# Eight resident Toeplitz tiles in a decoder layer's state-space mixer, with the selects, the row stores and the entry loads re-ordered

## The chip, the cores and the metric

One core of one Trainium2 chip runs the whole layer in one launch. The metric is device time in microseconds, from the run's own clock; lower is better. The engines are called as in the profile: PE (TensorE matmul), DVE (VectorE), ACT (ScalarE), POOL (GpSimd) and SP (SyncE, which only issues transfers here). All arithmetic is fp32 or fp32r.

## What is computed

The input x is 4 sequences of 1024 tokens by 256 channels. The layer has three blocks, each with a layer norm ahead and a residual behind it: a diagonal state-space mixer, cross attention to 64 context rows per sequence, and a feed-forward part (256 to 1024, two 1024 by 1024 layers, back to 256).

```python
def mixer(x):                                  # residual + (scan output) @ W_out.T + b_out
    xn = (x - mean) / sqrt(var + 1e-5) * ln_gamma + ln_beta
    dA = exp(-exp(log_A) * dt[:, None]); dB = B_param * dt[:, None]     # (256, 64)
    def step(h, u):
        h = dA * h + dB * u[..., None]
        return h, einsum('dn,bdn->bd', C_param, h) + D_param * u
    ys = scan(step, 0, xn)
    return x + einsum('btd,ed->bte', ys, W_out) + b_out
x = x + mixer(layernorm(x))
x = x + attention(ctx, ctx, layernorm(x))
x = x + ffn(layernorm(x))
```

## The kernel before

The scan is done in chunks of 64 steps (L = 64, 16 chunks a sequence, 64 columns in all). For each of the 256 channels (128 on the upper and 128 on the lower half of the partitions) there are three small products: `state` multiplies the tokens of a chunk by the channel's entries EE (64 x 64 powers of the decay) and gives what the chunk adds to the state; `within` multiplies the tokens by a 64 x 64 lower Toeplitz tile TT of the channel's convolution kernel; `carried` multiplies the scanned states by GG and adds them to the same output. Sixteen channels of each half are a group (GRP = 16, NGRP = 8), eight are a round (`OCT` = 8, 16 rounds); DVE runs the scan over the chunks of a round (L431).

**Preparation (0 to about 51 us).** DVE builds the powers GG by six doublings (L337), PE sums each column of GG over the 64 states with a row of ones (L461, four rounds v into four banks, each emptied by ACT, L277), and the sums, the convolution kernel, go to DRAM (`kernel_rows`, L175, eight stores of SP). From there SP loads the Toeplitz tiles: one transfer per half and group, 64 partitions that each read 4 KB one element further on (L141, `tt_load`). The entries come in the same way from `alpha_rows` (L146, `entries_load`) and ACT makes exponentials of them (L289). POOL clears what is above the diagonal of a Toeplitz tile with two selects a group (L211, `mask`). The tokens are normed twice over: DVE takes the statistics (L343, L346), POOL the power -0.5 (L240, L244), ACT and DVE scale and shift 20 and 12 columns of each half of the tokens (L284, L370), and DVE multiplies by gamma and adds beta in eight parts (L379, L384; `PARTS`), three of them ahead of the first product, the rest between the scans.

**Core (about 53 to 102 us).** PE goes through rounds o = 0 to 16. In a round it does state(o+1), within(o) and carried(o-1), 48 matmuls (96 records in the trace). Before round o it waits for: the selects of the group (`t_mask`), the exponentials (`e_rdy`), three, four, six and eight parts of the tokens (`z_b`), the scan of the round before (`h_scan`) and free output banks (`y_out`). Between the scans DVE does one gamma or beta pass a round up to o = 8. ACT empties the outputs (L304) and makes the residual bases (L292), to which POOL adds the bias `bo` (L216, needs `wo_in`, the landing of `bo` and `woT`).

**Order of the transfers.** One queue, SP's, issues nearly all: x, the two alpha stores, the tokens, gamma and beta, EE of groups 0 and 1, `bo`, `woT`, the row stores (each waits for ACT's copy), three small weights, then, once all rows are in DRAM (`kr_st`), TT of groups 0 to 3, EE of groups 2 to 7, the context rows. TT of groups 4 to 7 go into the same four buffers of `ring` and are each issued when PE has finished with the group four before (`w_ps`). POOL's queue runs: pow, pow, selects of group 0, pow, selects of groups 1 to 3, small masks, clearing of the value rows (L867), then `gpsimd_core` with selects 4 to 7 and the biases.

**Rest.** After the core PE turns and projects the outputs, takes part in the first attention block and runs the feed-forward loop (159 to 932 us); the weights are loaded in the shadow of this once the last state product is done (`h_ps`, L191 to L200). The change does not touch it.

Of the kernel before, what the change touches and what calls it, by code (L numbers as in the profile page):

```python
# [32 lines left out]
P = 128  # L33
BATCH, T, DM = 4, 1024, 256
N = 64
# [19 lines left out]
ACT_SHARE = 20  # L55
# [3 lines left out]
def mixer_parts(nc, ctx, a, t):  # L59
# [7 lines left out]
    def sem(name):  # L67
# [12 lines left out]
    ones = sb("ones", [P, 32], "c")  # L80
# [22 lines left out]
    dtc = sb("dtc", [P, 4], "d")  # L103

    TT = [ring[:, 1024 * k:1024 * (k + 1)] for k in range(4)]
    ksb = ring[:, :].rearrange("p (a m) -> p a m", a=8)
# [7 lines left out]
    kps = [[pair[k][:, 512 * h:512 * (h + 1)] for h in range(2)] for k in (2, 0)]  # L114
# [4 lines left out]
    x_in, E_in, xr_in = ([sem(f"m_{n}{g}") for g in range(8)] for n in ("x_in", "E_in", "xr_in"))  # L119
    const, exps, coef, al_st, coef_t, pk_done, g_row, d_add = (  # L120
        sem("m_" + n) for n in ("const", "exps", "coef", "al_st", "coef_t", "pk_done", "g_row", "d_add"))
    k_ps, k_ev, kr_pad, e_rdy, t_mask = (sem("m_" + n) for n in ("k_ps", "k_ev", "kr_pad", "e_rdy", "t_mask"))
    kr_st = sem("m_kr_st")
    T_in = [sem(f"m_T_in{k}") for k in range(4)]
# [24 lines left out]
    def sync_mixer(e):  # L149
# [20 lines left out]
        for v in range(4):  # L170
            for h in range(2):
                u = 2 * v + h
                e.wait_ge(k_ev, u + 1)
                c = (1 - h) * (P * L) + v * 2048
                e.dma_start(kr[0, c:c + 2048].rearrange("(q m) -> q m", q=4), ksb[0:P:32, u, :]).then_inc(kr_st, 16)  # L175
        for n in ("xW", "keys", "scl"):
            e.dma_start(t[n], a[n]).then_inc(k_in, 16)
        e.wait_ge(kr_st, 128)
        e.wait_ge(kr_pad, 16)
        for g in range(4):  # L180
            tt_load(e, g)
        for g in range(2, NGRP):
            entries_load(e, g)

    def sync_core(e):
        for g in range(4, NGRP):
            e.wait_ge(w_ps, 2 * (g - 4) + 2)
            tt_load(e, g)
# [4 lines left out]
        e.wait_ge(w_d, 48)  # L193
        for n in ("w1", "w2", "w3"):
            e.dma_start(t[n].bitcast(F32), t["d" + n]).then_inc(w_in, 16)
# [22 lines left out]
    def gpsimd_prep(e):  # L218
        e.memset(ident[:, :], 0.0).then_inc(const, 1)
        e.memset(rev[:, :], 0.0).then_inc(const, 1)  # L220
        e.memset(ones[:, :], 1.0).then_inc(const, 1)
# [4 lines left out]
        e.wait_ge(const, 6)  # L226
        e.affine_select(out=ident[:, :], in_=ident[:, :], compare_op=ALU.not_equal, fill=1.0, base=0,
                        pattern=[[-1, P]], channel_multiplier=1).then_inc(const, 1)
        for h in range(2):
            blk = rev[64 * h:64 * h + 64, 64 * h:64 * h + 64]  # L230
            e.wait_ge(const, 7 + h)
            e.affine_select(out=blk, in_=blk, compare_op=ALU.not_equal, fill=1.0, base=-63,
                            pattern=[[1, 64]], channel_multiplier=1).then_inc(const, 1)
        e.wait_ge(const, 9)
        e.dma_start(kr[:, DM * L:DM * L + L], rev[0:1, L:2 * L]).then_inc(kr_pad, 16)

        for b in range(2):
# [3 lines left out]
        mask(e, 0)  # L241
        e.wait_ge(t_mask, 2)
        e.wait_ge(nat_v, 1)
        e.tensor_tensor(rsm[:, :], svn[:, :], mhalf[:, :], ALU.pow).then_inc(natural, 1)  # L244
        e.wait_ge(natural, 1)
        for g in range(1, 4):
            mask(e, g)
        e.wait_ge(t_mask, 8)

    def gpsimd_core(e):  # L250
        e.wait_ge(wo_in, 32)
        done = 0
        for g, until in ((4, 0), (5, 0), (6, 0), (7, 4), (None, TILES)):
            for tile in range(done, until):
                bias(e, tile)
            done = until
            if g is not None:
                e.wait_ge(base_b, done)
                mask(e, g)
                e.wait_ge(t_mask, 2 * g + 2)  # L260

    def scalar(e):
# [11 lines left out]
        def row_evac(v):  # L274
            e.wait_ge(k_ps, v + 1)
# [17 lines left out]
        for v in range(4):  # L293
            row_evac(v)
        e.wait_ge(const, 9)
        norm_apply(0)
        entry_exp(0)
        norm_apply(1)
        for g in range(1, 3):
# [21 lines left out]
    def vector(e):  # L321
        e.wait_ge(exps, 2)
# [8 lines left out]
        for row in (0, N):  # L331
            e.tensor_copy(edit[row:row + 1, 1, :], wT[row:row + 1, :]).then_inc(d_add, 1)
# [6 lines left out]
        def stats(first, until):  # L339
            for j in range(first, until):  # L340
                if j % 4 == 0:
                    e.wait_ge(xr_in[j // 4], 16)
                e.bn_stats(stn[:, j, :], xres[:, j, :]).then_inc(stat, 1)  # L343
                if j % SB >= 2:
                    e.wait_ge(stat, j - 1)
                    e.bn_aggr(mvn[:, j - 2, :], stn[:, j - 2, :]).then_inc(aggr, 1)  # L346

        def variances(b):
            for j in (SB * b + SB - 2, SB * b + SB - 1):
                e.wait_ge(stat, j + 1)  # L350
                e.bn_aggr(mvn[:, j, :], stn[:, j, :]).then_inc(aggr, 1)
            e.wait_ge(aggr, SB * b + SB)
# [37 lines left out]
        stats(4, 8)  # L390
        double(5)
        e.wait_ge(d_in, 32)
# [1134 lines left out]
```

## Time and profile before

| | us |
|---|---|
| median of 3 runs | 935.07 (934.67 to 935.14) |
| the profiled execution | 934.08 |
| its span, first to last instruction | 932.3 |
| preparation, to the first `within` product | 53.0 |
| core, 53.0 to 102.4 | 49.4 |
| turn, project, first attention block, to 158.9 | 56.5 |
| feed-forward loop, to 932.3 | 773.4 |

The page has the busy share of each engine in 40 slices of 23.3 us: PE is at 99% from the sixth slice on, and below it in the first three, which hold the preparation and the core. The time line gives instructions in order of time with the idle time before them in square brackets; the chain of waits follows the end of the program back to what released each step, and "issue" in it is time for which the profile shows no cause. The windows give busy time, granted clock of TensorE, share of the 16 DMA engines and GB/s for a stretch.

### The profile page before, as it was taken

How to read it: one execution, taken by the hardware profiler on the slowest of the kernel's cores; microseconds unless marked ns; L12 is line 12 of the kernel's file. 1: busy time of each engine (PE TensorE's matmuls, PEld its weight loads, DVE VectorE, ACT ScalarE, POOL GpSimd, SP SyncE). 2: the span in 40 equal slices, each digit the busy share in tenths (PEclk: the TensorE clock that was granted, in tenths of full speed). 3: DMA queues.
4: the chain of work that ended last, by engine and by line, in shares of the span. 5: the costliest groups of instructions: out<-in, count | busy, mean ns of one | idle time of the engine just before them, and what ended most of it. 6: DMA issues, size and time to landing. Idle time of an engine off the chain costs nothing.

```text
span 932.3 us, 15096 instructions
## 1 busy us (share of the span) xinstructions
PE 869.6 (93%) x5570; PEld 697.0 (75%) x5570; DVE 514.6 (55%) x927; ACT 493.6 (53%) x761; POOL 183.2 (20%) x201
## 2 busy tenths in 40 slices
PE   1168999899999999999999999999999999999997
PEld 0068867677777778777877887778778777777886
DVE  7987485465446464555555555554555456553411
ACT  2927533476356735764475536653575366635432
POOL 1567800500041002200230014000500050003000
PEclk9679999999999999999999999999999999999999
DMA  9961797500110002000200010001100110001000
GB/s 340 243 162 55 261 387 306 226 1 1 52 45 0 0 22 73 0 0 15 81 0 0 0 73 22 0 0 51 45 0 0 51 45 0 0 23 45 1 1 25
DMA packets 15497, 61.79 MB, mean 66 GB/s; under 512 B 2835, under 2 KB 4502, under 8 KB 14646
## 3 DMA queue, kind: packets, MB, share of 16 engines
q1 hardware_dynamic: 15430, 61.31, 19.0%
q8 instruction: 24, 0.39, 0.2%
q14 instruction: 11, 0.09, 0.0%
q0 software_dynamic: 32, 0.00, 0.0%
HBM read 49.63 MB, written 23.20 MB: 78 GB/s over the span
## 4 chain that ended last, share of the span: by engine, by line
PE 89%; DVE 5%; issue 4%; ACT 1%; POOL 0%; DMA 0%; SPq 0%; DVEq 0%; POOLq 0%
PE pair L1342 51%; PE pair L1329 11%; PE pair L1354 6%; PE pair L1269 4%; PE pair L1280 3%; PE pair L1296 3%; PE pair L470 2%; PE pair L477 2%; PE pair L1289 1%; PE pair L1319 1%; PE pair L1236 1%; PE pair L484 1%; PE pair L539 1%; DVE GG L337 1%; DVE stn L343 1%
## 5 line engine op out<-in xcount | busy, mean ns | idle before, releaser
L950 ACT ACTIVATE vbuf<-pair,scl 128x512 f32<-128x512 f32 x128 | 87.8, 686 | 231.0 <-PE pair L1342 222.1
L1342 PE MATMUL pair<-h2hi,h_turned 128*128 128x512 f32 x512 | 202.6, 396 | 0.0
L1342 PE MATMUL pair<-h2lo,h_turned 128*128 128x512 f32 x512 | 199.6, 390 | 0.0
L1342 PE MATMUL pair<-h1hi,h_turned 128*128 128x512 f32 x384 | 153.1, 399 | 0.0
L1342 PE MATMUL pair<-h1lo,h_turned 128*128 128x512 f32 x384 | 150.0, 391 | 0.0
L1118 DVE TENSOR_TENSOR h1lo<-vbuf,h1hi 128x512 fp32r<-128x512 f32 x80 | 57.7, 722 | 120.1 <-ACT h1hi L951 119.3
L1342 PEld LDWEIGHTS pair<-h2hi,h_turned 128*128 128x128 f32 x512 | 96.2, 188 | 25.2 <-issue 5.9
L1342 PEld LDWEIGHTS pair<-h2lo,h_turned 128*128 128x128 f32 x512 | 96.2, 188 | 19.3
L1118 DVE TENSOR_TENSOR h2lo<-vbuf,h2hi 128x512 fp32r<-128x512 f32 x64 | 44.2, 691 | 107.2 <-ACT h2hi L951 107.1
L1329 PE MATMUL pair<-zThi,w_turned 128*128 128x512 f32 x224 | 92.0, 411 | 2.9 <-DVE vbuf L1142 2.9
L1142 DVE SCALAR_TENSOR_TENSOR vbuf<-pair,scl,sg 128x512 f32<-128x512 f32 x64 | 47.9, 750 | 80.5 <-ACT sg L939 60.8
L1342 PEld LDWEIGHTS pair<-h1hi,h_turned 128*128 128x128 f32 x384 | 72.1, 188 | 24.5 <-issue 10.5
L1329 PE MATMUL pair<-zTlo,w_turned 128*128 128x512 f32 x224 | 88.6, 396 | 0.0
L903 ACT ACT_TABLE_LOAD x65 | 83.4, 1283 | 1.1
L843 POOL TENSOR_TENSOR lnv<-lnv 128x4 f32<-128x4 f32 x16 | 16.3, 1017 | 342.8 <-DVE lnv L1023 320.4
L1342 PEld LDWEIGHTS pair<-h1lo,h_turned 128*128 128x128 f32 x384 | 72.2, 188 | 14.1
L875 POOL TENSOR_TENSOR h1lo<-vbuf,h1hi 128x512 fp32r<-128x512 f32 x48 | 61.9, 1290 | 79.6 <-ACT h1hi L942 79.6
L939 ACT ACTIVATE sg<-pair,scl 128x512 f32<-128x512 f32 x64 | 44.0, 687 | 58.9 <-PE pair L1329 57.7
L470 PE MATMUL pair<-tok,EE 64*64 64x60 f32 x512 | 38.7, 278 | 25.9 <-DVE tok L384 24.4
L1329 PEld LDWEIGHTS pair<-zThi,w_turned 128*128 128x128 f32 x224 | 42.6, 190 | 17.7 <-DVE vbuf L1142 7.4
L857 POOL TENSOR_TENSOR kblk<-keys,hmask 128x256 f32<-128x256 f32 x18 | 10.7, 616 | 207.6 <-PE pair L1269 207.6
L1342 PE MATMUL pair<-h1hi,w_turned 128*128 128x512 f32 x128 | 50.4, 394 | 0.0
(145 smaller groups left out, 1593.3 us busy)
## 6 DMA issues: line engine op xcount, KB each, us to landing
h_turned<-d_h SPq DMA_DIRECT2D x2, 4096.0 KB, 15.1
xres<-in_x SPq DMA_DIRECT2D x8, 512.0 KB, 7.5
tok<-in_xs SPq DMA_DIRECT2D x8, 512.0 KB, 12.2
EE<-alpha_rows SPq DMA_DIRECT2D x16, 256.0 KB, 10.7
ring<-kernel_rows SPq DMA_DIRECT2D x16, 256.0 KB, 4.3
xr<-x_rows SPq DMA_DIRECT2D x8, 512.0 KB, 3.5
out<-xr SPq DMA_DIRECT2D x16, 256.0 KB, 2.1
x_rows<-xres SPq DMA_DIRECT2D x7, 512.0 KB, 12.4
```

The costliest lines, as they stand in the source:

```text
L470: ins = e.matmul(out, EE[L * h:L * h + L, i, :], rhs, start=True, stop=True)
L875: e.tensor_tensor(h1[1][:, m, :], vb[:, m % 2, :], h1[0][:, m, :], ALU.subtract).then_inc(S["lo"], 1)
L903: e.activation(warm[:, 1:2], warm[:, 0:1], function).then_inc(S["warm"], 1)
L939: e.activation(sg[:, m % 2, :], pair[m % 2][:, 0:512], ACT.Silu, scale=sc1[:, m:m + 1]).then_inc(S["sg_rdy"], 1)
L950: e.activation(vb[:, s % 2, :], h_ps[s % 4], ACT.Gelu, scale=sc)
L1118: e.tensor_tensor(dst[1][:, n % HC, :], vb[:, n % 2, :], dst[0][:, n % HC, :], ALU.subtract).then_inc(S["lo"], 1)
L1142: e.scalar_tensor_tensor(vb[:, m % 2, :], pair[m % 2][:, 512:1024], sc2[:, m:m + 1], sg[:, m % 2, :], ALU.mult, ALU.mult).then_inc(S["v_rd ...
L1269: ins = e.matmul(pair[2][:, g * BLK + b * 256:g * BLK + (b + 1) * 256], qa[64 * g:64 * g + 64, h, tile * P:(tile + 1) * P], kblk[64 * g:64 ...
L1280: ins = e.transpose(pair[3][:, b * BLK + r * P:b * BLK + (r + 1) * P], unit(j, u)[:, r // 2, c:c + P], ident[:, :])
L1329: ins = e.matmul(pair[m % 2][:, 512 * g:512 * g + 512], w[:, k, m * P:(m + 1) * P], zT[part][:, k * BLK:(k + 1) * BLK], start=(k == 0 and ...
L1342: ins = e.matmul(bank, w[:, k, m * P:(m + 1) * P], src[part][:, k, :], start=(k == 0 and part == 0), stop=(k == HC - 1 and part == 1))
L1354: ins = e.matmul(h_ps[m], h1T[:, k, m * P:(m + 1) * P], h1[part][:, k, :], start=(k == 0 and part == 0), stop=(k == HC - 1 and part == 1))
```

## The change

- **Eight resident tiles.** TT of groups 4 to 7 get buffers of their own in the space of the weights w1 and w2, so no TT load waits for PE. All eight groups are loaded before the core. The loads of w1 to w3 into SBUF wait for the last `within` product.
- **SP's order.** EE of groups 0 to 3 are loaded ahead of the row stores; then TT 0, 1, 2, EE 4, TT 3, EE 5, TT 4, EE 6, TT 5, EE 7, TT 6, TT 7; `bo`, `woT` and the three small weights stand behind all of them.
- **POOL's order.** All selects move into `gpsimd_core`, behind its wait for `wo_in` and a new one for the third gamma pass (`z_h`), ahead of all biases and of the value rows' clearing. POOL also takes over the two one-row additions of D to GG and the two one-row copies back from DVE.
- **Kernel rows.** A weight `pick` with one column of ones places the four rounds in four rows of the same two banks, so PE does its 32 matmuls without a wait, ACT copies two tiles in place of eight, and stores eight times from its own queue, in the middle of its first norm pass (`ROWS_AT` = 3).
- **Work shared otherwise.** ACT takes the statistics of tiles 8 to 15 (two passes with an accumulated output, L295 and L301 of the changed kernel) and 18 in place of 20 columns of a norm pass, DVE 14 in place of 12. DVE clears the state banks at the start and does norms(1) after two whole parts of the tokens. All three first exponentials come after both norm passes. PE does five 128 x 512 matmuls (L497 of the changed kernel) after the second beta pass, ahead of the first state product, whose result is not used.

POOL's queue from the second pow to the value rows, before (`ring` holds TT, `rsm` and `rn` are the powers, the names in brackets the semaphores waited for):

```order
L240 TENSOR_TENSOR rn<-sv,mhalf 128x16 [waits m_sv_rdy] x2
L211 AFFINE_SELECT ring<-ring 64x1024 [waits m_t_mask,m_T_in0]
L211 AFFINE_SELECT ring<-ring 64x1024 [waits m_t_mask]
L244 TENSOR_TENSOR rsm<-svn,mhalf 128x32 [waits m_nat_v,m_t_mask]
L211 AFFINE_SELECT ring<-ring 64x1024 [waits m_t_mask,m_T_in1,m_natural]
```

and now:

```order
L250 TENSOR_TENSOR GG<-GG,edit 1x128 [waits m_g_row,m_w_row,m_d_in]
L250 TENSOR_TENSOR GG<-GG,edit 1x128
L244 TENSOR_TENSOR rn<-sv,mhalf 128x16 [waits m_sv_rdy,m_d_add]
L256 COPY GG<-edit 1x128 [waits m_powd,m_k_ps]
L256 COPY GG<-edit 1x128
L244 TENSOR_TENSOR rn<-sv,mhalf 128x16 [waits m_sv_rdy,m_g_back]
L261 TENSOR_TENSOR rsm<-svn,mhalf 128x32 [waits m_powd,m_nat_v]
```

```order
L213 AFFINE_SELECT ring<-ring 64x1024 [waits m_xr_T_in0,m_z_h,m_t_mask,m_wo_in,f_mk]
L213 AFFINE_SELECT ring<-ring 64x1024 [waits m_t_mask]
L213 AFFINE_SELECT ring<-ring 64x1024 [waits m_t_mask,m_xr_T_in1]
```

The first select has moved behind all three powers and waits for `m_wo_in` too, which it did not before.

SP's queue from the entries to the context rows, before:

```order
L146 DMA EE<-alpha_rows 64x1024 [waits m_al_st]
L146 DMA EE<-alpha_rows 64x1024 x3
L168 DMA bo<-in_ab 128x256
L169 DMA woT<-in_aW 128x512
L175 DMA kernel_rows<-ring 4x512 [waits m_k_ev] x8
L177 DMA xW<-in_xW 128x512
L177 DMA keys<-in_keys 128x512
L177 DMA scl<-in_scl 128x34
L141 DMA ring<-kernel_rows 64x1024 [waits m_kr_pad,m_kr_st]
L141 DMA ring<-kernel_rows 64x1024 x7
L146 DMA EE<-alpha_rows 64x1024 x12
```

and now (`tt_82` and `tt_83` are the buffers of groups 4 to 7):

```order
L154 DMA EE<-alpha_rows 64x1024 x7
L149 DMA ring<-kernel_rows 64x1024 [waits m_kr_pad,m_kr_st]
L149 DMA ring<-kernel_rows 64x1024 x5
L154 DMA EE<-alpha_rows 64x1024 x2
L149 DMA ring<-kernel_rows 64x1024 x2
L154 DMA EE<-alpha_rows 64x1024 x2
L149 DMA tt_82<-kernel_rows 64x1024 x2
L154 DMA EE<-alpha_rows 64x1024 x2
L149 DMA tt_82<-kernel_rows 64x1024 x2
L154 DMA EE<-alpha_rows 64x1024 x2
L149 DMA tt_83<-kernel_rows 64x1024 [waits m_nat_v]
L149 DMA tt_83<-kernel_rows 64x1024 x3
L184 DMA bo<-in_ab 128x256
L185 DMA woT<-in_aW 128x512
```

`bo` and `woT` have gone from ahead of the row stores to behind 24 transfers of 256 KB that wait for the rows.

The diff, cut to what the text speaks of:

```diff
-ACT_SHARE = 20
+ACT_SHARE = 18
+ACT_STATS = (8, 16)
+ROWS_AT = 3
+PAD = L
...
-    kps = [[pair[k][:, 512 * h:512 * (h + 1)] for h in range(2)] for k in (2, 0)]
+    kps = [pair[2][:, 512 * h:512 * (h + 1)] for h in range(2)]
...
-        for g in range(2):
+        for g in (0, 1, 2, 3):
             entries_load(e, g)
+        e.wait_ge(kr_st, 128)
+        e.wait_ge(kr_pad, 16)
+        for g in range(NGRP):
+            if g == 6:
+                e.wait_ge(nat_v, 1)
+            tt_load(e, g)
+            if g in (2, 3, 4, 5):
+                entries_load(e, g + 2)
         e.dma_start(bo[:, :], a["ab"].partition_broadcast(P)).then_inc(wo_in, 16)
         e.dma_start(woT[:, :, :], a["aW"]).then_inc(wo_in, 16)
...
     def sync_core(e):
-        for g in range(4, NGRP):
-            e.wait_ge(w_ps, 2 * (g - 4) + 2)
-            tt_load(e, g)
         e.wait_ge(h_ps, NOCT)
...
     def gpsimd_core(e):
         e.wait_ge(wo_in, 32)
-        done = 0
-        for g, until in ((4, 0), (5, 0), (6, 0), (7, 4), (None, TILES)):
...
+        e.wait_ge(z_h, 3)
+        for g in range(NGRP):
+            mask(e, g)
+        e.wait_ge(t_mask, 2 * NGRP)
+        for tile in range(TILES):
+            bias(e, tile)
...
+        def row_evac():
+            e.wait_ge(k_ps, 1)
             for h in range(2):
-                e.activation(ksb[:, 2 * v + h, :], kps[v % 2][h], ACT.Copy).then_inc(k_ev, 1)
+                e.activation(ksb[:, h, :], kps[h], ACT.Copy).then_inc(k_ev, 1)
+            for h in range(2):
+                e.wait_ge(k_ev, h + 1)
+                for v in range(4):
+                    c = (P * (1 - h) + 32 * v) * PAD
+                    e.dma_start(kr[0, c:c + 32 * PAD].rearrange("(q m) -> q m", q=4), ksb[v:P:32, h, :]).then_inc(kr_st, 16)
...
             for c in range(2 * SB * b, 2 * SB * b + ACT_SHARE):
+                if c == ROWS_AT:
+                    row_evac()
...
         gamma(0)
-        norms(1)
         beta(0)
         gamma(1)
         beta(1)
+        norms(1)
         gamma(2)
...
-                    ins = e.matmul(kps[v % 2][h][32 * q:32 * q + 32, :], ones[N * h:N * h + N, 0:32], GGf[N * h:N * h + N, c:c + 8 * L], start=True, stop=True)
-            ins.then_inc(k_ps, 1)
+                    ins = e.matmul(kps[h][32 * q:32 * q + 32, :], pick[N * h:N * h + N, 3 - v:35 - v], GGf[N * h:N * h + N, c:c + 8 * L], start=(v == 0), stop=(v == 3))
+        ins.then_inc(k_ps, 1)
+        e.wait_ge(pk_done, 7)
+        e.wait_ge(w_row, 2)
+        e.wait_ge(z_b, 2)
+        for _ in range(5):
+            e.matmul(pair[3][:, 0:BLK], ident[:, :], GGf[:, 0:BLK], start=True, stop=True)
...
-        m["gpsimd_core"](e)
```

## Rows read from the trace of the kernel before

**Rows 1.** The page's second part: busy tenths in 40 slices.

```profile
PE   1168999899999999999999999999999999999997
DMA  9961797500110002000200010001100110001000
```

**Rows 2.** Windows: length, busy (records) by engine, PEclk, DMA share, GB/s.

```profile
53.00:102.40 49.40, 43.63 (x1512) 42.23 (x1508) 35.30 (x78) 29.27 (x53) 36.10 (x45) 0.92 0.34 93
102.40:158.90 56.50, 51.92 (x304) 41.92 (x305) 36.67 (x62) 20.04 (x27) 11.94 (x17) 1.00 0.98 371
158.90:932.30 773.40, 765.25 (x3666) 609.34 (x3664) 395.87 (x661) 416.46 (x621) 113.16 (x118) 1.00 0.07 27
```

**Rows 3.** The chain of waits: start, length, what.

```profile
49.33 2.05 DVE tok L384
...
51.43 1.86 PE pair L470 x30
...
57.12 2.79 issue
...
71.29 1.25 issue
...
83.58 1.51 issue
```

**Rows 4.** Time line of DVE, 47 to 80 us (x4: four parts of one scan).

```profile
47.14 2.15 DVE L379 TENSOR_TENSOR tok<-tok,gam 128x1024 f32<-128x1024 f32 x1
...
61.53 1.35 DVE L431 TENSOR_TENSOR_SCAN scan<-dec,pair 128x128 f32<-128x128 f32 x4 [2.17 <-PE pair L484]
...
64.63 1.35 DVE L431 TENSOR_TENSOR_SCAN scan<-dec,pair 128x128 f32<-128x128 f32 x4 [0.63 <-PE pair L484]
65.90 1.20 DVE L379 TENSOR_TENSOR tok<-tok,gam 128x1024 f32<-128x1024 f32 x1
67.22 1.35 DVE L431 TENSOR_TENSOR_SCAN scan<-dec,pair 128x128 f32<-128x128 f32 x4
...
78.36 2.09 DVE L379 TENSOR_TENSOR tok<-tok,gam 128x1024 f32<-128x1024 f32 x1
```

**Rows 5.** Time line of POOL, 38 to 109 us.

```profile
38.70 2.37 POOL L211 TENSOR_SCALAR_AFFINE_SELECT ring<-ring 64x1024 f32<-64x1024 f32 x2 [4.27 <-DMA ring<-kernel_rows]
46.75 11.05 POOL L211 TENSOR_SCALAR_AFFINE_SELECT ring<-ring 64x1024 f32<-64x1024 f32 x6
...
78.24 3.22 POOL L211 TENSOR_SCALAR_AFFINE_SELECT ring<-ring 64x1024 f32<-64x1024 f32 x2 [2.89 <-DMA ring<-kernel_rows]
...
87.82 19.34 POOL L216 TENSOR_TENSOR xres<-xres,bo 128x256 f32<-128x256 f32 x28
107.11 1.20 POOL L857 TENSOR_TENSOR kblk<-keys,hmask 128x256 f32<-128x256 f32 x2
```

**Rows 6.** Time line of SP's queue, 18 to 50 us: start, issuing time, transfer.

```profile
18.68 0.59 SPq L168 DMA_DIRECT2D bo<-in_ab  x1
19.30 0.91 SPq L169 DMA_DIRECT2D woT<-in_aW  x1
23.09 5.65 SPq L175 DMA_DIRECT2D kernel_rows<-ring  x8
...
34.03 4.96 SPq L141 DMA_DIRECT2D ring<-kernel_rows  x8
39.03 7.63 SPq L146 DMA_DIRECT2D EE<-alpha_rows  x12
```

**Rows 7.** Windows of 1 us: length, PEclk, DMA share, GB/s.

```profile
24.00:25.00 1.00, 1.00 1.04 411
25.00:26.00 1.00, 1.00 1.14 303
26.00:27.00 1.00, 1.00 1.08 241
...
32.00:33.00 1.00, 0.50 0.98 354
33.00:34.00 1.00, 0.50 0.27 72
34.00:35.00 1.00, 0.50 0.01 1
35.00:36.00 1.00, 0.50 0.60 217
36.00:37.00 1.00, 0.50 1.05 254
...
57.00:58.00 1.00, 0.94 1.06 224
58.00:59.00 1.00, 1.00 0.23 52
```

**Rows 8.** The page's DMA issues: transfer, count, KB each, median us to landing.

```profile
woT<-in_aW SPq DMA_DIRECT2D x1, 256.0 KB, 13.3
out<-xr SPq DMA_DIRECT2D x16, 256.0 KB, 2.1
```

**Rows 9.** Time line of PE and ACT around the kernel rows, 20 to 26 us.

```profile
20.42 6.59 PE L461 MATMUL pair<-GG,ones 64*32 64x512 f32 x64 [14.60 <-DVE GG L397]
22.47 1.08 ACT L277 ACTIVATE ring<-pair 128x512 f32<-128x512 f32 x2 [13.49 <-PE pair L461]
24.18 1.08 ACT L277 ACTIVATE ring<-pair 128x512 f32<-128x512 f32 x2 [0.62 <-PE pair L461]
```

**Rows 10.** Traffic by queue, first of 50 to 57 us, then of 57 to 59 us.

```profile
q1 hardware_dynamic: 523, 1.68, 103.6%
...
q1 hardware_dynamic: 292, 0.26, 60.1%
q8 instruction: 1, 0.02, 3.9%
```

**Rows 11.** Windows of 2 us in the core: length, busy by engine, PEclk, DMA share, GB/s.

```profile
62.00:64.00 2.00, 2.00 (x64) 2.00 (x62) 2.00 (x4) 1.10 (x2) 0.00 (x0) 0.52 0.57 176
66.00:68.00 2.00, 2.00 (x83) 2.00 (x80) 1.88 (x4) 0.85 (x2) 1.91 (x1) 1.00 0.00 0
```

More of the change, by code:

```diff
@@ L240, in gpsimd_prep @@
             e.tensor_tensor(rn[:, 0, here], sv[:, here], mhalf[:, 0:SB], ALU.pow).then_inc(powd, 1)
-        mask(e, 0)
-        e.wait_ge(t_mask, 2)
+        e.wait_ge(d_in, 32)
+        e.wait_ge(w_row, 2)
+        e.wait_ge(g_row, 7)
+        for row in (0, N):
+            v = GG[row:row + 1, :, L - 1]
+            e.tensor_tensor(v, v, edit[row:row + 1, 0, :], ALU.add).then_inc(d_add, 1)
+        e.wait_ge(d_add, 2)
+        power(0)
+        e.wait_ge(k_ps, 1)
+        e.wait_ge(powd, 1)
+        for row in (0, N):
+            e.tensor_copy(GG[row:row + 1, :, L - 1], edit[row:row + 1, 1, :]).then_inc(g_back, 1)
+        e.wait_ge(g_back, 2)
+        power(1)
         e.wait_ge(nat_v, 1)
+        e.wait_ge(powd, 2)
         e.tensor_tensor(rsm[:, :], svn[:, :], mhalf[:, :], ALU.pow).then_inc(natural, 1)
         e.wait_ge(natural, 1)
-        for g in range(1, 4):
-            mask(e, g)
-        e.wait_ge(t_mask, 8)
     def gpsimd_core(e):
         e.wait_ge(wo_in, 32)
-        done = 0
-        for g, until in ((4, 0), (5, 0), (6, 0), (7, 4), (None, TILES)):
[L254 to L260, printed above, removed]
+        e.wait_ge(z_h, 3)
[4 more added lines that the diff above has]
+            bias(e, tile)
     def scalar(e):
@@ L292, in residual_base @@
             e.activation(xres[:, j, :], xres[:, j, :], ACT.Identity, bias=ngn[:, j:j + 1], scale=rsn[:, j:j + 1]).then_inc(base, 1)
-        for v in range(4):
-            row_evac(v)
-        e.wait_ge(const, 9)
+        for first in range(*ACT_STATS, 4):
+            tile_stats(first, first + 4)
+        e.wait_ge(const, 10)
         norm_apply(0)
-        entry_exp(0)
         norm_apply(1)
-        for g in range(1, 3):
+        for g in range(3):
             entry_exp(g)
@@ L321, in vector @@
     def vector(e):
+        for k in range(2):
+            e.memset(hps[k], 0.0).then_inc(h_zero, 1)
+        e.memset(dec[:, :, 0], 0.0).then_inc(dec0, 1)
         e.wait_ge(exps, 2)
@@ L343, in stats, with last_two @@
                 e.bn_stats(stn[:, j, :], xres[:, j, :]).then_inc(stat, 1)
+                n = j if j < SB else j - (ACT_STATS[1] - ACT_STATS[0])
                 if j % SB >= 2:
-                    e.wait_ge(stat, j - 1)
+                    e.wait_ge(stat, n - 1)
                     e.bn_aggr(mvn[:, j - 2, :], stn[:, j - 2, :]).then_inc(aggr, 1)
+        def last_two(b):
+            until, n = (ACT_STATS[0], TILES)[b], ACT_STATS[0] + SB * b
+            for j in (until - 2, until - 1):
+                e.wait_ge(stat, n - (until - 1 - j))
+                e.bn_aggr(mvn[:, j, :], stn[:, j, :]).then_inc(aggr, 1)
         def variances(b):
[L349 to L352, printed above, removed]
+            if b == 0:
+                e.wait_ge(t_var, ACT_STATS[1] - ACT_STATS[0])
+            e.wait_ge(aggr, ACT_STATS[0] + SB * b)
             here = slice(SB * b, SB * b + SB)
@@ L476, in within @@
                 rows = slice(L * h, L * h + L)
-                ins = e.matmul(yps[o % 4][rows, c * BC:(c + 1) * BC], TT[o // 2 % 4][rows, (i % GRP) * L:(i % GRP + 1) * L], tok[rows, :, i], start=(c == 0), stop=False)
+                ins = e.matmul(yps[o % 4][rows, c * BC:(c + 1) * BC], TT[o // 2 % 8][rows, (i % GRP) * PAD:(i % GRP) * PAD + L], tok[rows, :, i], start=(c == 0), stop=False)
             return ins
```

111 lines of the change are left out of this document (55 added, 56 removed).

## The prediction

> **What bounds the kernel now.** The slices of the page [rows 1] come first: PE is full from the sixth slice on, so only the first 102 us can move much. The windows [rows 2] cut the program in stages; the last two, 56.5 and 773.4 us, follow the core's end by PE's own work and are not touched, so what the core's end gains or loses arrives at the end one for one. In the chain [rows 3] the first `within` product comes at 53.0, behind DVE's third beta pass (49.33) and 1.86 us of state products; DVE is the engine that sets the start. In the core, PE is busy 43.6 of 49.4 us, and the three pauses called "issue", 2.79 + 1.25 + 1.51 = 5.55 us, are nearly all of the rest. They wait for no semaphore. The traffic by queue [rows 10] shows what they are: no instruction packet from 50 to 57 us, and one in the 2 us after that, as the transfers run out (DMA share 1.06, then 0.23 [rows 7]); PE resumes at 59.91. PE's program is loaded by the same DMA engines, and a piece came late behind data.
>
> Before the core those engines are the second thing to read [rows 7]: full up to 33 us, empty at 34, full again from 36 to 58. Tokens move at 411 GB/s, entries and Toeplitz tiles at 241 to 254 GB/s only. `woT`, issued at 19.30 [rows 6], landed 13.3 us later [rows 8]: a load lands when everything queued before it on SP's queue has gone.
>
> **The change, part by part.**
>
> *Start of the chain.* DVE loses eight tiles of statistics, the one-row work and the bank clearing, some 5 us ahead of its gamma passes; ACT gains the statistics in time in which it was idle (it had waited 13.49 us at 22.47 [rows 9]). The four matmul rounds, 1.71 us apart by ACT's copies (22.47 to 24.18 [rows 9]), take 4 x 1.71 + 0.3 = 7.2 us in a row. They start about when they did (20.4): the last doubling ends a little earlier, POOL's two additions take 1 us where DVE took 0.8. So the sums are there at 27.6 and copied at 28.7, 1.08 for two copies. Eight stores follow on ACT's queue. No row has a transfer issued by ACT. Below, it could cost ACT nothing; above, the 0.65 of SP's (5.65 / 8, waits included [rows 6]); I take 0.5 each, so the last is issued near 32.7.
>
> *When the rows are in DRAM.* Entries 0 to 3 are eight transfers of 256 KB ahead of the stores. One takes 1.10 us: between 35.3 and 57.3 us twenty went (8 + 12 [rows 6]; from the first traffic at 35 to the end at 58 less 0.26 MB of context rows [rows 7]). They begin when the tokens end, at 25.3 (the rate falls from 411 to 303 and 241), and end at 25.3 + 8.8 = 34.1. The stores land behind that, 0.8 us later (traffic ended at 33.2, SP went on at 34.03): 34.9. I take 35.0 against 34.03 before. With stores that cost ACT nothing and pass the entries it would be 31.5; with 0.65 each and 2.1 us to land [rows 8], 36.
>
> The Trainium skill (DMA: Bandwidth & Descriptors, "Queues, rings and completion order") says that each DMA engine goes round between the queues it has work for, packet by packet. By that rule ACT's stores would not wait for SP's entries, and the pause at 57.12 speaks against it for code; by the rule the rows would be there near 34.5.
>
> *The long queue.* From then on SP issues 24 transfers of 256 KB, 16 of tiles and 8 of entries, and then `bo` and `woT`. First traffic comes 1.3 us after SP goes on (34.03 to 35.3): 35.0 + 1.3 + 24 x 1.10 = 62.7. `bo` and `woT` are 0.39 MB; the small loads at 30 to 33 us ran at about 280 GB/s (311, 354 and less), so 1.4 us more, and 0.8 to the semaphore: **`wo_in` at 64.9**. Issuing isn't the limit: 24 x 0.62 (4.96 / 8) is 15 us.
>
> *The new wait.* POOL's first select now waits for `wo_in`, and PE's round 0 for that select. Before, `wo_in` came at 33 and nothing of the kind stood ahead of group 0, whose selects ran at 38.70 [rows 5]. Queued behind the waiting POOL are all 16 selects, the biases, the value rows. Two selects take 2.37 us when DVE is quiet [rows 5]: round 0 starts at 67.3 in place of 53.0, **+14.3 us**. All that was gained on DVE and ACT ahead of it comes to nothing: even if the third gamma pass came 5 us sooner or later than my 48, it is long over. The five extra matmuls and the first state products run in this shadow, and the clock that they warm has fallen by 67: in 30 to 57 us, PE idle, it was granted at 0.50, the level of 1.2 GHz [rows 7].
>
> *The core itself.* A round took 3.1 us at half clock and 2.6 at full (scans at 61.53, 64.63, 67.22 [rows 4], with 0.52 and 1.00 granted [rows 11]). Minus: the three pauses, since by 67 only small loads are left, -5.55; half a round's worth of clock after the pause at 57, -0.4; shorter contention in single rounds, -0.6. Plus: all 16 selects now run beside DVE's gamma and beta passes. Such a pass takes 1.20 us alone and 2.09 to 2.15 beside selects [rows 4, 5], a select 1.18 and 1.84 (11.05 / 6). DVE then needs 1.27 + 2.1 + 0.1 = 3.45 us a round against PE's 2.6, for about seven rounds until the selects end near 90. By the waits (scan o-1 before round o, the scan behind the last pass) the first 2.5 us of lag are hidden: 7 x 0.85 - 2.5 = +3.4. Bounds: 0, if selects and passes interleave, and +6. Sum -3.2 us: the core takes 46.2.
>
> *Behind the core.* POOL's 32 biases at 0.69 (19.34 / 28 [rows 5]) run from 90 to 112, the key masks at 113. Before, they were done at 108.3 and first needed near 116, 14 us after the core's end; now needed near 127. Cover enough: nothing. If it were gone, each bias late costs 0.69. The loads of w1 to w3 wait for the last `within`, but they waited for their own first leg 12 us longer anyway: nothing.
>
> **Sum.** +14.3 - 3.2 = +11.1 us on the profiled execution's 934.08: **945.2**. That execution lies 1.0 below the median of 935.07, so I leave the forecast at the sum and the range a little open above.
>
> **Rivals.**
>
> *A. Selects without contention.* As forecast, but the passes stay near 1.2 us: +7.7, 941.8. For it: single passes at 1.20 [rows 4]. Against it: every pass that lay beside a select was slower. With the early bound for the rows (31.5: the tiles then follow the entries at 34.1 without a gap, -2.2) it is 939.6; with +6 and rows at 36, 948.8. These are the range of the forecast.
>
> *B. The hold is not `wo_in` but PE's code.* Were `wo_in` in time, round 0 could start at 53, but PE's next piece of program, asked for around 52, would stand behind the 24 transfers as it stood behind the entries before. Then PE went on at 59.91, 2.6 us after the last entries at 57.3; now it would pause in round 1 until 62.7 + 2.6 = 65.3: +5.4, less 2.8 for the two later pauses, plus about 1 of contention: +3.6, 937.7.
>
> *C. The other side: the loads overtake.* If `woT` landed soon after its issue, the change would do what its order allows. SP issues it at 35.0 + 24 x 0.62 + 1.5 = 51.4; with 2.1 to land and 2.37 of selects round 0 starts at 55.9, +2.9, and -3.2 in the core: 933.8. Only with rows at 31.5 too is it 930.3, faster. It decides at about 53 us for `wo_in`. Against it: 13.3 us for `woT` at a shorter backlog [rows 8].
>
> **Chances.** Forecast 0.55 and A 0.32 (one mechanism, 939.6 to 948.8), B 0.05, C 0.08, of which half is faster. The range 940.0 to 949.0 leaves out B, C and the outermost of A. A measurement of this kernel can tell 0.2%, 1.9 us, from no change. Faster 0.04, the same 0.04, slower 0.92.
>
> **What would show it.** POOL's first select at about 65, idle before it, released by the landing of `woT`; DMA share near 1.0 without a gap from 4 to 64 us; PE's first `within` near 67, the state products some 15 us before; no "issue" pause over 0.5 us in the core; gamma and beta passes of 2.1 us; core 46 us, the rest 56.5 and 773 as before. Wrong it would be if `wo_in` came before 55, or if PE's rounds waited for something else, such as code.

## The result, and the profile after

| | before | after |
|---|---|---|
| median, us | 935.11 (934.67 to 937.21, 4 runs) | 946.7 (945.08 to 949.25, 4 runs) |
| ratio | 1 | 1.0132, 95% interval 1.0112 to 1.0152 |
| profiled execution, us | 934.08 | 947.29 |
| its span, us | 932.3 | 945.6 |
| round 0 starts | 53.0 | 69.0 |
| core, us | 49.4 | 46.2 |
| behind the core, us | 56.5 + 773.4 | 56.5 + 773.9 |

The changed kernel is 1.3% slower. The page's second part, 40 slices of 23.6 us, answers to [rows 1]: the third slice of PE has fallen to 2 tenths.

```profile
PE   1229999899999999999999999999999999999997
DMA  9880299610020002000110011001100110001000
```

The windows of the changed kernel by stage, as [rows 2] (length, busy time and records of PE, PEld, DVE, ACT and POOL, granted clock, DMA share, GB/s). The first row is new: 16 us in which PE does nothing and the DMA engines are full. The core is shorter than before by 3.2 us, and the two stages behind it are the same within 0.5 us.

```profile
53.00:69.00 16.00, 0.01 (x2) 0.01 (x2) 1.89 (x4) 0.00 (x0) 2.29 (x2) 0.59 0.95 239
69.00:115.20 46.20, 43.25 (x1504) 41.87 (x1504) 34.59 (x72) 29.50 (x53) 44.79 (x46) 0.96 0.08 27
115.20:171.70 56.50, 51.92 (x304) 41.94 (x305) 36.67 (x62) 20.03 (x27) 8.15 (x13) 1.00 0.98 368
171.70:945.60 773.90, 765.30 (x3666) 609.29 (x3664) 395.96 (x661) 416.13 (x621) 113.02 (x118) 1.00 0.08 27
```

SP's queue in the changed kernel, as [rows 6]: it stands from 21.4 to 36.69 for the rows, and `woT` is its 26th transfer after that.

```profile
16.19 5.22 SPq L154 DMA_DIRECT2D EE<-alpha_rows  x8
36.69 3.64 SPq L149 DMA_DIRECT2D ring<-kernel_rows  x6
...
52.52 0.43 SPq L185 DMA_DIRECT2D woT<-in_aW  x1
```

POOL's time line in the changed kernel, as [rows 5], with the idle time and its releaser in brackets: the first select came after 28.55 us of waiting, released by `woT` and not by a Toeplitz tile.

```profile
66.57 11.69 POOL L213 TENSOR_SCALAR_AFFINE_SELECT ring<-ring 64x1024 f32<-64x1024 f32 x8 [28.55 <-DMA woT<-in_aW]
78.39 13.26 POOL L213 TENSOR_SCALAR_AFFINE_SELECT tt<-tt 64x1024 f32<-64x1024 f32 x8
91.73 24.08 POOL L218 TENSOR_TENSOR xres<-xres,bo 128x256 f32<-128x256 f32 x32
```

The chain of waits of the changed kernel, as [rows 3], carries the transfer of `woT` and the two selects behind it where DVE's third beta pass stood:

```profile
52.52 13.94 DMA woT<-in_aW
66.50 0.08 issue
66.57 1.16 POOL ring L213
67.74 0.06 issue
67.79 1.15 POOL ring L213
```

### The profile page after: what moved, and what is told of

Read it like the earlier page. It is cut to its first block, busy times and chain, and to the rows that moved or that the text cites. A ratio compares the mean times of both kernels' runs of the same rounds, so it can differ in the third digit from the quotient of the medians.

```text
span 945.6 us, 15135 instructions
## 1 busy us (share of the span) xinstructions
PE 876.2 (93%) x5580; PEld 699.6 (74%) x5580; DVE 508.7 (54%) x909; ACT 497.7 (53%) x789; POOL 184.9 (20%) x206
## 4 chain that ended last, share of the span: by engine, by line
PE 86%; issue 4%; POOL 3%; DVE 3%; DMA 2%; SPq 2%; ACT 1%; ACTq 0%; POOLq 0%; DVEq 0%
PE pair L1377 50%; PE pair L1364 11%; PE pair L1389 6%; PE pair L1304 4%; PE pair L1315 3%; PE pair L1331 3%; DMA woT<-in_aW 1%; PE pair L1324 1%; PE pair L1354 1%; POOL tt L213 1%; PE pair L1271 1%; POOL ring L213 1%; PE pair L574 1%; PE pair L505 1%; SPq L149 1%
## 6 DMA issues: line engine op xcount, KB each, us to landing
x_rows<-xres SPq DMA_DIRECT2D x7, 512.0 KB, 13.2
```

## The experiments

Ratios are to the kernel before, run in the same rounds, with 95% intervals. 0.001 is 0.93 us.

### 1. Move the wait, or move the loads

Two cures of the same hold (the time for which round 0 is kept waiting). The first moves POOL's wait:

```diff
     def gpsimd_core(e):
-        e.wait_ge(wo_in, 32)
         e.wait_ge(z_h, 3)
         for g in range(NGRP):
             mask(e, g)
         e.wait_ge(t_mask, 2 * NGRP)
+        e.wait_ge(wo_in, 32)
```

> The changed kernel, with POOL's wait for the landing of the output weights moved behind the sixteen selects, ahead of the biases; SP's order is untouched. Theory (the wait holds round 0 and nothing else): POOL's first select starts when the third gamma pass is done, 48.0 in the changed kernel; two selects of 2.37 us at the least, 3.7 beside DVE's passes; round 0 at 51 to 53 in place of 69.0. The tiles of group g land ahead of their selects (TT 0 near 40, TT 7 near 64). Core 46 to 48 us as before the edit, so the core ends 14 to 16.5 us earlier: 930.5 to 933.5 on the changed kernel's 946.7, that is 0.2 to 0.5% faster than the kernel before. Rival B of the prediction (PE's code is stuck behind the 24 transfers): round 0 starts at 52 but an issue pause in round 0 or 1 lasts until near 65; +3.6 against the kernel before, 937 to 939. Third possibility: the code loads come amid the backlog, but late by a few us in all (the packet at 55.27 in the changed kernel came while the backlog lasted to 67): 933 to 937.

The second leaves the wait and moves the two loads of `bo` and `woT` ahead of `e.wait_ge(kr_st, 128)`:

> The changed kernel with bo and woT issued ahead of the Toeplitz tiles (behind the entries of groups 0 to 3), POOL's wait left where it is. If the place of these two loads on SP's queue is what makes the wait long, it comes out as the other cure of the same hold: wo_in near 36 instead of 65, first select at 48, round 0 at 51 to 54; the 24 transfers follow 1.4 us later, which nothing waits for. Within 1.5 us of the variant with the wait behind the selects: 930.5 to 935. If the selects' move behind the third gamma pass is what costs (not the loads), it stays near 946.

Measured: 1.0014 (1.0003 to 1.0025) and 1.0020 (1.0006 to 1.0033). They agree, so the hold is `wo_in`, and it costs 1.1 to 1.2%, some 11 us. But 14 to 16.5 were expected. Waits of PE in the first variant, 50 to 116 us (total, times, longest), and its chain:

```profile
PE pair L512 <- issue: 4.1, 2, 3.7
PE pair L519 <- issue: 2.3, 1, 2.3
...
PE pair L505 <- POOL ring L213: 0.3, 1, 0.3
```

```profile
55.09 2.30 issue
61.97 3.70 issue
```

Round 0 started at 51.88, 17 us sooner, as expected. Then PE stood twice without a semaphore (the second variant has the same two pauses, 1.74 and 4.79 us). The windows of the same run (columns as above) show the rest of the price: DMA share 1.0 up to 66 us, and a granted clock near 0.50, the level of 1.2 GHz, behind each pause.

```profile
54.00:56.00 2.00, 1.09 (x43) 0.91 (x35) 2.00 (x6) 0.00 (x0) 1.87 (x2) 1.00 1.03 238
...
58.00:60.00 2.00, 2.00 (x67) 2.00 (x61) 1.21 (x4) 0.64 (x2) 1.80 (x3) 0.52 1.01 240
...
62.00:64.00 2.00, 0.00 (x0) 0.00 (x0) 0.07 (x1) 0.00 (x0) 1.93 (x2) 1.00 1.01 234
...
66.00:68.00 2.00, 2.00 (x69) 2.00 (x66) 1.29 (x5) 0.60 (x1) 1.87 (x2) 0.50 0.88 240
```

Its traffic by queue from 54 to 58 us has one packet of program in the midst of 291 of data:

```profile
q1 hardware_dynamic: 291, 0.96, 102.9%
q8 instruction: 1, 0.02, 2.1%
```

The trace dates these packets, 16 KB each on queue q8. All 21 pauses of 0.7 us or more in which PE waited for no semaphore, in the profiles of all runs here, ended 1.3 to 1.7 us after the end of such a packet. Five of them:

| run | packet begins, us | takes | PE goes on | after its end |
|---|---|---|---|---|
| before | 57.31 | 1.25 | 59.91 | 1.35 |
| wait moved | 54.49 | 1.33 | 57.40 | 1.58 |
| wait moved | 63.06 | 1.32 | 65.67 | 1.29 |
| loads moved | 55.77 | 1.24 | 58.42 | 1.41 |
| loads moved | 64.29 | 1.29 | 66.97 | 1.39 |

The packet itself takes no longer than some do beside idle DMA engines (0.9 to 1.5). What is late is its start: 8.6 us passed between the two starts in the first variant, where 3.4 and 3.5 us passed late in the core before (93.16, 96.56, 100.06). So the third possibility held: the pieces are not stuck until the backlog ends, each comes late by itself. (The expectations of experiments 1 and 3 date three packets some 0.3 us later than the trace.)

### 2. Without the five idle matmuls

The first cure, less the loop of five matmuls at L497.

> The variant with the wait behind the selects, but without PE's five 128x512 matmuls ahead of the first state product. If they pay by the clock: before the core PE is idle from 27 to 50, the first rounds then run at the granted 0.50 (a round 3.1 instead of 2.6 us) for two or three rounds, 1 to 2 us slower than with them. If DVE's pitch of 3.35 us sets the first rounds anyway, they are worth nothing: within 0.5 us of the variant with them. They take 7.4 us ahead of the first state product (43.2 to 50.5); if the first state product waits for them rather than for the third beta pass, leaving them out gains up to 1 us.

Measured 1.0023 (1.0006 to 1.0040), not to be told from 1.0014. The first state product came 0.8 us sooner (48.88 against 49.71), round 0 by 0.2 (51.66), as much as DVE's first gamma pass began sooner in that execution (37.45 against 37.66); pauses of 2.55 and 4.44 us followed. The windows settle what the five matmuls do to the clock. First without, then with them:

```profile
52.00:54.00 2.00, 2.00 (x85) 2.00 (x81) 2.00 (x3) 0.00 (x0) 1.93 (x2) 0.50 1.03 225
```

```profile
52.00:54.00 2.00, 2.00 (x78) 2.00 (x82) 2.00 (x5) 0.00 (x0) 1.93 (x2) 1.00 1.02 231
```

They raise the granted clock of the first rounds from 0.50 to 1.00. Whether that is worth any time here isn't settled by the ratios.

### 3. Pace the loads

The first cure, and the second half of the long queue issued by PE's progress:

```diff
-        for g in range(NGRP):
-            if g == 6:
-                e.wait_ge(nat_v, 1)
-            tt_load(e, g)
-            if g in (2, 3, 4, 5):
-                entries_load(e, g + 2)
+        for g in range(4):
+            tt_load(e, g)
+            if g == 2:
+                entries_load(e, 4)
...
     def sync_core(e):
+        for n, load, g in ((1, entries_load, 5), (2, tt_load, 4), (3, entries_load, 6), (4, tt_load, 5),
+                           (5, entries_load, 7), (6, tt_load, 6), (7, tt_load, 7)):
+            e.wait_ge(w_ps, n)
+            if n == 6:
+                e.wait_ge(nat_v, 1)
+            load(e, g)
```

> The variant with the wait behind the selects, with the second half of the long queue paced: TT 0 to 3 and EE 4 go as before, and EE 5, TT 4, EE 6, TT 5, EE 7, TT 6, TT 7 are each issued only when PE has finished within-round 1, 2, 3, 4, 5, 6, 7. Theory now on trial: in the variant without the hold PE stood for 2.3 us (55.1) and 3.7 us (62.0) without a semaphore, because its pieces of program (packets at 54.8 and 63.4) came late through DMA engines full to 67 us; with ten transfers in place of 24 ahead of the core they are empty from about 51, and the pieces come in time. Round 0 stays at 52, both pauses go, and so do the clock's falls behind them (0.52 and 0.50 granted for 2 to 3 us each): 6 to 7 us less, core end at 96 to 97, 928 to 930, ratio to the kernel before 0.994 to 0.996. Rival: the pauses come from the program's own loading (its size, other engines' code), not from data; then they stay and so does the time, 935.5.

Measured 0.9971 (0.9958 to 0.9983): 4 us less than unpaced, the first version here that beats the kernel before. In its windows the DMA engines are free from 54 us, 0.9 us after PE began the core (53.14), and PE works through where it stood before:

```profile
54.00:56.00 2.00, 2.00 (x82) 2.00 (x79) 2.00 (x4) 0.00 (x0) 1.93 (x2) 0.50 0.02 5
...
62.00:64.00 2.00, 2.00 (x82) 2.00 (x76) 2.00 (x6) 0.52 (x1) 1.87 (x2) 1.00 0.48 156
```

PE's second program packet began 4.6 us after the first (53.98, 58.61) and not 8.6. But the expected 6 to 7 us were too many. Shorter pauses stay beside the paced transfers (these are PE's waits, 50 to 116 us). POOL's selects hold round 0 for 1.2 us, and behind that wait the clock still fell, to 0.50 in the first window above. Round 0 itself started 1.3 us later than unpaced, as did DVE's first gamma pass (38.93 against 37.66): a difference between executions, not of the edit.

```profile
PE pair L516 <- issue: 2.7, 3, 1.4
PE pair L509 <- POOL ring L217: 1.2, 1, 1.2
PE pair L509 <- issue: 0.8, 2, 0.4
```

Then the same idea on the kernel before, which has nothing of the change:

```diff
         for g in range(4):
             tt_load(e, g)
-        for g in range(2, NGRP):
+        for g in range(2, 4):
             entries_load(e, g)
...
         for g in range(4, NGRP):
+            e.wait_ge(w_ps, 2 * (g - 4) + 1)
+            entries_load(e, g)
             e.wait_ge(w_ps, 2 * (g - 4) + 2)
             tt_load(e, g)
```

> The kernel before, with nothing of the change, but with the entries of groups 4 to 7 paced: each issued when PE has finished within-round 1, 3, 5, 7, in turn with the tiles of groups 4 to 7, which waited so already. If the pause of 2.79 us at 57.12 in the kernel before is PE's program behind 20 transfers, 12 transfers are gone by 49 and it goes: 2 to 3.5 us faster, ratio 0.9965 to 0.998. The two later pauses, 1.25 and 1.51 us, may stay, since two transfers go out near them. Rival, the pause has another cause: 0. It also says how much of the paced variant's gain needs the change at all.

Measured 0.9979 (0.9970 to 0.9989). The pause of 2.79 us at 57 [rows 3] is gone; the longest is now 1.75 us at 64.2, beside paced transfers. The profiled execution, the slowest of its twelve, had 4.8 us of pauses in all, hardly less than before, so the gain is known from the times and where it arises is seen only at that first pause. By the times, pacing is worth 2 us without the change and 4 us with the hold cured, and what the rest of the change brings to a paced kernel, 0.9971 against 0.9979, can't be told from nothing.

### 4. The one part alone, on the kernel before

```diff
-        e.dma_start(bo[:, :], a["ab"].partition_broadcast(P)).then_inc(wo_in, 16)
-        e.dma_start(woT[:, :, :], a["aW"]).then_inc(wo_in, 16)
         for v in range(4):
...
         for g in range(2, NGRP):
             entries_load(e, g)
+        e.dma_start(bo[:, :], a["ab"].partition_broadcast(P)).then_inc(wo_in, 16)
+        e.dma_start(woT[:, :, :], a["aW"]).then_inc(wo_in, 16)
...
     def mask(e, g):
+        e.wait_ge(wo_in, 32)
...
-        mask(e, 0)
-        e.wait_ge(t_mask, 2)
...
-        for g in range(1, 4):
+        for g in range(4):
             mask(e, g)
```

> The kernel before, with the one part of the change that the forecast holds to be its cost: bo and woT issued behind the entries of groups 2 to 7, and the selects, with the power of 32 columns ahead of them, behind the landing of both. By the working of the prediction: the last entries land at 57.3, bo and woT 1.4 us later, 0.8 to the semaphore, selects 2.37: round 0 at 62 in place of 53.0, +9; the pause at 57 has no cover left, -2.8; six more selects beside DVE's passes, +1 to +2: 7 to 9 us slower, 941 to 944, ratio 1.0075 to 1.0095. If the wait did not matter by itself it would be near 1.000.

Measured 1.0077 (1.0057 to 1.0098), within the band. Round 0 started at 64.4 (62 was expected), after this transfer in its chain:

```profile
48.04 13.82 DMA woT<-in_aW
```

The core took 47.3 us. The pause of 2.79 us is not in it, and those of 1.26 and 1.54 us are.

### 5. Selects beside DVE's passes

The changed kernel with its hold, but selects that clear one tile of 16 in groups 1 to 7, and biases only behind the last beta pass. It leaves out most of the clearing of the Toeplitz tiles.

```diff
+            n = GRP if g == 0 else 1
-            v = TT[g][L * h:L * h + L, :].rearrange("p (d t) -> p d t", d=GRP)
+            v = TT[g][L * h:L * h + L, 0:n * L].rearrange("p (d t) -> p d t", d=n)
...
+        e.wait_ge(z_b, 8)
         for tile in range(TILES):
```

> The changed kernel, hold included, but the selects of groups 1 to 7 clear only the first of the 16 tiles of a group (64x64 instead of 64x1024), and the biases wait for the last beta pass, so that POOL is quiet beside DVE's passes. This leaves out most of the clearing of the Toeplitz tiles. It measures the contention term alone. Theory of the forecast (passes of 2.1 us beside selects set a DVE pitch of 3.35 us): passes fall to 1.2 us, the pitch of the scans in the first half to PE's 2.6 to 2.9, the core from 46.2 to about 42.5: 942 to 944. Rival A of the prediction (selects cost DVE nothing that counts): unchanged within 0.5 us, 946.5. In both the biases may become late: 32 x 0.75 us after the last beta pass end near 113, as now.

> The changed kernel itself once more, on the same chip and in the same rounds as the variant with thin selects, to compare the two directly. 1.0132 [1.0112, 1.0152] to the kernel before, as the first time.

> The variant with thin selects once more (the changed kernel with only the first of 16 tiles cleared in groups 1 to 7, biases behind the last beta pass; it leaves out most of the clearing). Its first profile had a core of 42.3 us against 46.2, but its ratio of four executions, 1.0127, is hardly below the 1.0132 of the changed kernel. If the contention of selects with DVE's passes costs what the forecast's term says (+3.4 us, core 46.2 against 42.8), the ratio is 0.003 to 0.004 below that of the changed kernel in the same rounds; if what is gained in DVE's passes is lost again elsewhere (PE's program loads, which the faster core meets sooner), it is within 0.001 of it.

Measured 1.0127 (1.0102 to 1.0151) at first; then, in the same rounds, 1.0113 (1.0094 to 1.0132) against 1.0130 (1.0113 to 1.0147) of the changed kernel. The time lines show the mechanism. DVE in the changed kernel (its first profile; 2.16 for a pass, 3.35 from scan to scan):

```profile
78.45 2.16 DVE L422 TENSOR_TENSOR tok<-tok,gam 128x1024 f32<-128x1024 f32 x1
80.53 1.34 DVE L463 TENSOR_TENSOR_SCAN scan<-dec,pair 128x128 f32<-128x128 f32 x4
81.79 2.16 DVE L427 TENSOR_TENSOR tok<-tok,bet 128x1024 f32<-128x1024 f32 x1
83.88 1.34 DVE L463 TENSOR_TENSOR_SCAN scan<-dec,pair 128x128 f32<-128x128 f32 x4
```

and with thin selects (second profile; 1.20 and 2.59):

```profile
79.67 1.20 DVE L424 TENSOR_TENSOR tok<-tok,gam 128x1024 f32<-128x1024 f32 x1
80.99 1.35 DVE L465 TENSOR_TENSOR_SCAN scan<-dec,pair 128x128 f32<-128x128 f32 x4
82.26 1.20 DVE L429 TENSOR_TENSOR tok<-tok,bet 128x1024 f32<-128x1024 f32 x1
83.58 1.35 DVE L465 TENSOR_TENSOR_SCAN scan<-dec,pair 128x128 f32<-128x128 f32 x4
```

A select stretches a pass and not a scan, and not every pass. Two selects of the changed kernel, from its chain of waits, beside the rows above:

```profile
76.09 2.18 POOL ring L213
78.39 1.15 POOL tt L213
```

DVE's pass at 76.07 began 0.02 us ahead of the first of them: the pass took 1.19 and the select 2.18. The pass at 78.45 began 0.06 behind the second: the select took 1.15 and the pass 2.16. In these rows the one that begins second pays, so what a select costs DVE hangs on hundredths of a microsecond. (Once, in the second profile, a pass that began 0.05 behind a select kept its 1.19, and the select took 2.25.)

The cores took 42.2 and 41.8 us with thin selects, 46.2 and 43.8 with whole ones; 1.6 of the 46.2 are late rounds that have another cause (below). The term is worth 2 to 4 us by the profiles and 1.6 us by the ratios, whose intervals overlap. The edit also moved the biases. So the stretched passes are shown, the size of the term is not settled.

### 6. Better versions

The paced variant with selects 2 to 11 each behind a pass:

```diff
             e.wait_ge(t_mask, 2 * g + h)
+            k = 2 * g + h
+            if 2 <= k < 12:
+                e.wait_ge(z_b if h else z_h, 4 + (k - 2) // 2)
```

> As the paced variant, and POOL's selects 2 to 11 (of 16) each wait for a gamma or beta pass to be done, so that they lie beside DVE's scan and not beside the pass. If a select slows only a pass and not a scan (a scan took 1.35 us with and without selects), passes fall from 2.1 to 1.2 us, the pitch of the early rounds from 3.3 to about 2.7: 2 to 3.5 us less than paced, 925.5 to 928. If the gates make PE wait for selects instead, or the biases, 32 of 0.69 to 0.75 us behind the selects, end too late for the first attention block (needed at about 105), the gain is 0 or it is slower by 1 to 3 us.

Measured 0.9970 (0.9958 to 0.9982), the same as paced. The early scans came 2.4 to 2.6 us apart (52.59, 54.98, 57.55), and the passes beside them took 1.20 and not 2.16, so the gates work, but PE then stood without a semaphore for 3.9 us in five pauses. The two longest ended 1.4 us after the end of a program packet:

```profile
PE pair L519 <- issue: 3.9, 5, 1.9
```

Then the paced variant with the selects of group 0 behind the second beta pass (`z_b` at 2) and four idle matmuls:

> The paced variant (ratio 0.9971), with the selects of group 0 behind the second beta pass in place of the third gamma pass, so that they lie beside DVE's 14 scale-and-shift instructions, and four idle matmuls in place of five. In the paced variant round 0 waited 1.23 us for the selects, which ran beside gamma and beta passes, at 53.14, and the first state products waited for the five matmuls. Theory: round 0 starts 1.5 to 2.5 us earlier, near 51, and what is gained stays: ratio 0.9945 to 0.996. Rival: the pieces of PE's program, each loaded after the one before is used up, are the next bound; the earlier start then meets them earlier and the ratio stays within 0.001 of 0.997.

Measured 0.9987 (0.9974 to 0.9999), not better than paced and probably worse. The two selects stretched DVE's norms(1), which stands ahead of the third beta pass, from 3.67 to 5.46 us (DVE, this variant, then paced):

```profile
42.47 5.46 DVE L419 TENSOR_SCALAR tok<-tok,spread 128x128 f32<-128x128 f32 x14
```

```profile
43.73 3.67 DVE L417 TENSOR_SCALAR tok<-tok,spread 128x128 f32<-128x128 f32 x14
```

Round 0 began 1.1 us sooner (52.06 against 53.14), but DVE's first gamma pass had begun 1.3 us sooner in that execution (37.67 against 38.93), so the edit gained nothing at the start: the first state products now waited 1.7 us for the third beta pass. The theory failed there, and the rival, that an earlier start meets late pieces of program, was not tested by it. The cores ended at 100.5 and 100.6. Why the median came out 1.5 us higher stays open.

Last, both together, and EE of groups 4 and 5 ahead of the wait for the rows:

> As the variant with early group 0, with the gated selects (2 to 11 each behind a gamma or beta pass) and with EE 4 and 5 ahead of the wait for the rows, so that two transfers less go out in the core. The gated variant had quicker early rounds (scans 2.4 to 2.6 us apart) but five issue pauses of 3.9 us in all, and came out at 0.9970. Theory: less to load beside PE's program makes the pauses shorter: ratio 0.993 to 0.9955. Rival, as for the other: 0.996 to 0.998.

Measured 0.9951 (0.9932 to 0.9969), 930.2 us: the best of all, on the upper edge of what was expected, faster than the kernel before and than the changed one. Which of its parts does it was not taken apart. The interval of the paced variant overlaps it, so which of the two is better isn't settled.

## Why the prediction was right, point by point

- **Rows in DRAM**: 35.0 was forecast, SP went on at 36.69. The price of a store was not the fault. The forecast had the last of eight issued near 32.7, at 0.5 us each; it was out by 32.2, at a median of 0.49 (the first took 1.06):

```profile
27.11 5.07 ACTq L311 DMA_DIRECT2D kernel_rows<-ksb  x8
```

  (The upper bound of the forecast took 5.65 / 8 for 0.65; it is 0.71, which puts the bound for the rows near 36.5 and not 36.) What the sum had too early is the landing. It let the entries end at 34.1 and the rows land 0.8 us behind them. The DMA share did fall in that microsecond (0.91 from 33 us, 0.43 from 34, 0.09 from 35), but the last packet of the entries began at 35.6, and of the 64 packets of the stores (q10 is ACT's queue) one ran up to 33 us and 63 behind it, the last at 35.8. First 27 to 33 us, then 33 to 36.5:

```profile
q1 hardware_dynamic: 445, 1.45, 102.7%
q10 hardware_dynamic: 1, 0.00, 0.2%
```

```profile
q1 hardware_dynamic: 103, 0.31, 33.4%
q10 hardware_dynamic: 63, 0.06, 6.7%
```

  The trace does not show the even turn between queues that the Trainium skill states (DMA: Bandwidth & Descriptors, "Queues, rings and completion order"). The prediction had put the rows near 34.5 by that rule. A packet on another queue did begin under SP's backlog in experiment 1, that of the program at 54.49. What decides the delay was not measured.
- **The long queue**: from 36.69 on, 1.3 + 24 x 1.10 + 1.4 + 0.8 gives 66.6, and the first select came at 66.57. This term was exact; the 1.7 us of the rows went through it. In the second profile SP went on at the same 36.68, but the select came at 68.41: the drain took 1.8 us more in that execution, for which the sum had no term.
- **The new wait**: selects 2.42 us, forecast 2.37. Round 0 at 69.0 (second profile 70.8), forecast 67.3: +16.0 in place of +14.3. The other cure and the one part alone say the same of the cause.
- **The core**: 46.2 forecast, 46.2 measured, but the agreement is partly luck. The pauses went, as forecast (issue waits of 0.8 us in all against 5.55). Contention was there: four passes at 2.16, the others between 1.19 and 1.72, not seven at 2.1, because a pass that began ahead of its select was not stretched. That term was forecast at 3.4 us; by the second profiles of whole and thin selects it is 2.0. Beside it stood a term that nobody had forecast, slow late rounds (below), worth 1.6 us. The second profile, without them and with a little less contention, has a core of 43.8.
- **Behind the core**: 56.5 and 773.9; biases to 115.8 (112 forecast) and key masks at 116.4 (113) held nobody. As forecast.
- **Sum**: +13.2 us in the profiled execution against +11.1 forecast, of which 1.7 is the rows; +11.6 between the medians.
- **Rival A** is out as a mechanism (passes did take 2.16), though its price, 3.4 us less, is near what the thin selects gained. **Rival C** is out: `woT` landed 13.94 us after its issue. **Rival B** was the most useful to have written down: it was not the hold, but it was what stood behind it. It gave +3.6 us for a kernel with `wo_in` in time, and the two such kernels came out at 1.0014 and 1.0020, +1.3 and +1.9. Its picture, a piece that comes only when all 24 transfers are gone, was wrong: PE's pieces began at 54.5 and 63.1 under a backlog to 67, and it lost 6 us in two parts.

## What to carry to other kernels

A wait is as long as the queue ahead of the transfer that it waits for: before a wait is put ahead of other work, count what stands before that load on its queue, and put the wait directly ahead of the first instruction that reads the data. When such a hold is cured, look at once for what was hidden in it: here PE's program came through the same DMA engines as the bulk loads, and the gain came only when those were issued by PE's progress and not all at once. Work of POOL next to DVE was cheap here beside a scan and dear beside an elementwise pass that began after it, also when that pass is one that the start waits for.

## What the runs showed of the hardware

- PE, standing in a pause without a semaphore, went on 1.3 to 1.7 us after the end of a 16 KB packet of its program (21 pauses, table in experiment 1).
- A piece of PE's program took different times in two executions of one kernel, both beside nearly idle DMA engines. Traffic of the changed kernel from 95 to 112 us, first profile (four pieces in 2.0% of 16 engines' 17 us, 1.4 us each):

```profile
q8 instruction: 4, 0.07, 2.0%
```

  and second profile (five pieces, 0.9 us each):

```profile
q8 instruction: 5, 0.08, 1.7%
```

  The same three late rounds took 3.05 to 3.15 us from scan to scan in the first and 2.6 in the second. PE's busy time went with it, at a granted clock of 1.00 in both:

```profile
105.00:108.00 3.00, 2.77 (x101) 2.55 (x96) 1.35 (x4) 3.00 (x7) 3.00 (x5) 1.00 0.00 0
```

```profile
105.00:108.00 3.00, 3.00 (x121) 3.00 (x115) 1.76 (x6) 3.00 (x7) 3.00 (x6) 1.00 0.00 0
```

  In the first, PE also stood for 0.23 and 0.30 us up to 107.37 and 111.35, each 1.4 us after the end of a piece. That slow pieces cause the slow rounds is read from their coincidence. It is found again in the second profile with thin selects (pieces of 1.40 and 1.36, rounds of 2.96 and 2.86), but the first profile there has a round of 3.03 beside a piece of 1.09, and no run set the speed of a piece by itself.
- A store issued by ACT kept its queue busy for 0.49 us (median of eight; one of SP's in the kernel before, 0.48); the eight took 5.07 us out of ACT's first norm pass.
- A pass of DVE of 1.20 us took 2.16 when it began just behind a select, and one instruction (the scale of `rsn`) took 1.12 where it took 0.22 with thin selects, while a scan stayed at 1.35.
